# Attention's output matrix by seven products on pairs of node tiles, in a graph transformer on one Trainium2 core

## What is computed

```
for i in range(4):
    y = norm(x) * (1 + cond @ s1_w + s1_b) + cond @ b1_w + b1_b
    q, k, v = y @ wq + bq, y @ wk + bk, y @ wv + bv
    attn = softmax over the edges of q . k / sqrt(128), head by head
    x = x + (attn @ v) @ wo + bo
    y = norm(x) * (1 + cond @ s2_w + s2_b) + cond @ b2_w + b2_b
    x = x + relu(y @ m_w1 + m_b1) @ m_w2 + m_b2
```

## Time and profile before

| | us |
|---|---|
| median of 3 runs | 2349.93 (2349.65 to 2351.52) |
| the profiled execution's own time | 2344.98 |
| its span, first to last instruction | 2343.3 |
| TensorE busy | 2319.4 (99%) |
| VectorE busy | 1399.7 (60%) |
| ScalarE busy | 939.6 (40%) |
| GpSimd busy | 1098.8 (47%) |

### The profile page before, as it was taken

The page is one execution under the profiler, slowest core; times in us unless marked ns, Lnnn a source line. Parts: engine busy times, 40 slices in busy tenths (PEclk is TensorE's granted clock), DMA queues, the critical chain, the costliest instruction groups (busy, mean ns, idle before and its releaser), DMA issues. The chain is left out here.

```text
span 2343.3 us, 28395 instructions
## 1 busy us (share of the span) xinstructions
PE 2319.4 (99%) x9765; PEld 1465.6 (63%) x9765; DVE 1399.7 (60%) x2463; ACT 939.6 (40%) x1590; POOL 1098.8 (47%) x1482
## 2 busy tenths in 40 slices
PE   8999999999999999999999999999999999999999
PEld 4565655457676577777577777667767755544443
DVE  7777860524775663777564577565477655633445
ACT  4436642222764231666231376322266522312221
POOL 2005212041665481565384365466266543627775
PEclk9999999999999999999999999999999999999999
DMA  6411011420666210466210176510066611669517
GB/s 174 146 38 29 31 33 35 118 86 1 167 167 181 95 60 1 103 168 161 84 44 23 42 175 162 137 44 23 1 152 168 173 46 53 228 235 344 190 46 238
DMA packets 132367, 257.73 MB, mean 110 GB/s; under 512 B 49695, under 2 KB 51471, under 8 KB 129884
## 3 DMA queue, kind: packets, MB, share of 16 engines
q1 hardware_dynamic: 85294, 150.84, 21.7%
q0 software_dynamic: 45584, 102.75, 15.8%
q10 hardware_dynamic: 1346, 2.33, 0.4%
HBM read 213.17 MB, written 32.20 MB: 105 GB/s over the span
## 5 line engine op out<-in xcount | busy, mean ns | idle before, releaser
L115 POOL DMA_DIRECT2D cols<-w x720 | 354.1, 499 | 247.4 <-PE psum L1027 200.8
L1027 PE MATMUL psum<-cols,rows 125*128 125x256 f32 x1600 | 369.0, 379 | 0.0
L1014 PE MATMUL psum<-g_k_cols,g_q_cols 128*125 128x512 f32 (+1 forms) x960 | 360.8, 513 | 0.2
L1027 PEld LDWEIGHTS psum<-cols,rows 125*128 125x128 f32 x1600 | 303.2, 190 | 39.4 <-issue 3.8
L1133 DVE CUSTOM_DVE_ANT_0 g_prob<-psum,ln_count 125x1250 f32<-125x1250 f32 x160 | 233.8, 1461 | 101.3 <-PE psum L1014 100.9
L1014 PEld LDWEIGHTS psum<-g_k_cols,g_q_cols 128*125 128x125 f32 x960 | 179.4, 187 | 165.2 <-issue 155.5
L1231 ACT ACTIVATE g_prob<-g_prob,g_row_max 125x1250 f32<-125x1250 f32 x160 | 216.1, 1351 | 123.0 <-DVE g_row_max L1133 121.1
L1147 DVE STREAM_TRANSPOSE w<-g_prob 128x1280 f32<-128x1280 f32 x160 | 241.5, 1510 | 39.5 <-DMA cols<-w 26.8
L1237 ACT ACTIVATE g_prob<-g_prob,g_row_max 125x1250 f32<-125x1250 f32 x160 | 215.9, 1349 | 68.5 <-DVE g_row_max L1122 68.1
L3298 PE MATMUL psum<-m_ew,m_x_cols 128*64 128x256 f32 (+1 forms) x576 | 152.3, 498 | 0.0
L1040 PE MATMUL psum<-g_wo,g_q_cols 128*125 128x512 f32 x320 | 143.5, 593 | 0.0
(11 more groups left out here) (440 smaller groups left out, 4252.4 us busy)
## 6 DMA issues: line engine op xcount, KB each, us to landing
cols<-w POOLq DMA_DIRECT2D x720, 80.0 KB, 3.2
cols<-w SPq DMA_DIRECT2D x560, 80.0 KB
w<-in_L_gnn_m_w SPq DMA_DIRECT2D x8, 1024.0 KB
slot_rows<-p_kf SPq DMA_DIRECT2D x1, 7344.0 KB, 33.0
rows<-slot_rows SPq DMA_DIRECT2D x54, 136.0 KB
m_ew<-in_L_ffn_expert_w SPq DMA_DIRECT2D x4, 1536.0 KB, 12.6
slot_outputs<-slot_rows SPq DMA_DIRECT2D x1, 5000.0 KB
w<-in_L_mix_W SPq DMA_DIRECT2D x4, 1024.0 KB, 5.2
```

Of the source, the lines that this page charges most:

```text
L115: return eng.dma_start(out, in_, allow_slow_non_contiguous=True)
L1014: ins = pe.matmul(psum[0:P, at:at + width], q_cols[:, h, t * P:(t + 1) * P], k_cols[:, h, start:start + width], start=True, stop=True)
L1027: ins = pe.matmul(c.bank(6 + g % 2, 256).rearrange("p (u a i) -> p u a i", u=2, a=SIDE), rows[0:P, j, h * 128:(h + 1) * 128], turned_keys[ ...
```

## The change

`outputs` goes. `att_pe` takes its place in all four layers: the seven products of `mlp_pe`, on `wo`, with the attention's result in `q_cols` as the stationary side. The functions `mlp_*` that served the pairs are renamed `pair_*` and take a record, `att` or `mlp`, with the semaphores and the scratch; their work is the same. The norm behind attention follows the pairs' order (`by_pairs`), by `pair_stats_dve` and `apply_dve`. Sums of blocks are new: GpSimd makes those of `wo` behind the moves of pairs 11 to 14, and the first of each of two groups of node blocks behind those of 15 and 16; VectorE makes the rest for pair 0 ahead of the last transposition, for pairs 1 and 2 behind it; GpSimd makes those of pairs 3 and 4 after the parts of pairs 0 and 1. The sums of `m_w1` move behind the parts of pairs 2 and 3. `weigh` of pairs 18 and 19 stand in a row behind pair 0.

```diff
+    ATT_SUMS_AT = [(0, 0), (1, 0), (1, 1), (0, 0), (1, 0)]
+        k_all = k_cols[:].rearrange("p c n -> p (c n)")
+        att_weight_sums = [k_all[:, i * D:(i + 1) * D].rearrange("p (c o) -> p c o", c=2) for i in range(3)]
+        att_weight_sums.append(wo[:, 0:2, half_tile:D])
+        att_sums = [k_all[:, at:at + 8 * n].rearrange("p (i c n) -> p i c n", i=4, c=2)
+                    for at, n in ((3 * D, P), (3 * D + 8 * P, 2 * P))]
+        att = Pairs(0, o_mm, o_act_made, o_dve_made, o_pool_made, (0, 256, 512, 768, 1024, 1792, 2048, 2304))
+        mlp = Pairs(1, m_mm, m_act_made, m_dve_made, m_pool_made, range(0, 4 * D, half_tile))
...
-            return m % 2 == 1 and m < 2 * L - 1
+            return m < 2 * L - 1
...
+        def att_weight_sum_pool(l, n):
+            g = c.pool
+            a11, a21, a12, a22 = (wo[:, c0:c0 + 2, o:o + half_tile] for c0 in (0, 2) for o in (0, half_tile))
+            s1, s2, s3, s4 = att_weight_sums
+            if n == 0:
+                g.wait_ge(wo_in, 16 * KC * (l + 1))
+                g.tensor_tensor(s1, a21, a22, ALU.add).then_inc(o_weight_sums, 1)
...
+        def att_blocks(t0, t1, tiles=1):
+            return (q_cols[:, c0:c0 + 2, t * P:(t + tiles) * P] for c0 in (0, 2) for t in (t0, t1))
+        def att_first_sum_pool(l, slot):
+            g = c.pool
+            b11, b12, _, _ = att_blocks(slot, 3 + slot, 1 + slot)
+            if slot == 1:
+                g.wait_ge(out_made, PAIRS * l + PAIRS // 2)
+            g.tensor_tensor(att_sums[slot][:, 0], b12, b11, ALU.subtract).then_inc(o_sums_pool, 1)
+        def att_sums_dve(l, slot):
+            v = c.dve
+            _, b12, b21, b22 = att_blocks(slot, 3 + slot, 1 + slot)
+            t1, t2, t3, t4 = (att_sums[slot][:, i] for i in range(4))
+            v.wait_ge(out_made, PAIRS * l + NT // 2 * 3 + 2 + slot)
+            v.wait_ge(o_sums_pool, 10 * l + 2)
+            v.tensor_tensor(t2, b22, t1, ALU.subtract).then_inc(o_sums_dve, 1)
+            v.tensor_tensor(t3, b22, b12, ALU.subtract).then_inc(o_sums_dve, 1)
+            v.wait_ge(o_sums_dve, 6 * l + 3 * slot + 1)
+            v.tensor_tensor(t4, b21, t2, ALU.subtract).then_inc(o_sums_dve, 1)
+        def att_sums_pool(l, j):
+            g = c.pool
+            done = 10 * l + 4 * j - 10
+            b11, b12, b21, b22 = att_blocks(*VALUE_TILES[j])
+            t1, t2, t3, t4 = (att_sums[j - 3][:, i, :, 0:P] for i in range(4))
...
+        def att_pe(l, j, p):
+            pe = c.pe
+            n = VALUE_PAIRS * l + j
+            if p == 1:
+                if j == 0:
+                    pe.wait_ge(wo_in, 16 * KC * (l + 1))
+                    pe.wait_ge(score_read, STEPS * (l + 1) - 1)
+                    pe.wait_ge(out_made, PAIRS * l + NT // 2 * 3 + 2)
+                else:
+                    pe.wait_ge(o_act_made, 4 * n - 2)
+            elif p == 6:
+                if j == 0:
+                    pe.wait_ge(o_weight_sums, 4 * l + 4)
+                else:
+                    pe.wait_ge(o_dve_made, 3 * n)
+                if j < 2:
+                    pe.wait_ge(o_sums_dve, 6 * l + 3 * j + 3)
+                elif j >= 3:
+                    pe.wait_ge(o_sums_pool, 10 * l + 4 * j - 6)
+            elif p == 5 and j < 2:
+                pe.wait_ge(out_made, PAIRS * l + (PAIRS - 2 if j == 0 else PAIRS))
+            elif p == 7:
+                pe.wait_ge(o_dve_made, 3 * n + 1)
+            elif p == 3:
+                pe.wait_ge(o_act_made, 4 * n + 3)
...
+            ins.then_inc(o_mm, 1)
...
-            def outputs(t):
-                pe.wait_ge(out_made, PAIRS * l + 3 * NT // 2 + t // 2 + 1)
-                if t < 2:
-                    pe.wait_ge(score_read, STEPS * (l + 1) - 1)
-                else:
-                    pe.wait_ge(o_added, NT * l + t - 1)
-                for k in range(KC):
-                    ins = pe.matmul(c.bank(t % 2, D, P), q_cols[:, k, t * P:(t + 1) * P], wo[:, k, :],
-                                    start=(k == 0), stop=(k == KC - 1))
-                ins.then_inc(o_mm, 1)
-
...
-            pe.wait_ge(wo_in, 16 * KC * (l + 1))
-            outputs(0)
-            outputs(1)
-            weigh(PAIRS - 2, 0)
-            weigh(PAIRS - 2, 1)
-            pe.wait_ge(score_read, STEPS * (l + 1))
-            norm_pe(2 * l, 0)
-            norm_pe(2 * l, 1)
-            outputs(2)
-            weigh(PAIRS - 1, 0)
-            weigh(PAIRS - 1, 1)
-            for t in range(3, NT):
-                outputs(t)
-                if t == 3:
-                    pe.wait_ge(out_made, PAIRS * (l + 1))
-                norm_pe(2 * l, t - 1)
-            norm_pe(2 * l, NT - 1)
+            for j in range(VALUE_PAIRS):
+                for p in PAIR_ORDER:
+                    att_pe(l, j, p)
+                    if j >= 1 and p in (3, 4):
+                        norm_pe_turn(2 * l, 2 * j - (2 if p == 3 else 1))
+                if j == 0:
+                    pe.wait_ge(score_read, STEPS * (l + 1))
+                for t in (2 * j, 2 * j + 1):
+                    norm_pe_start(2 * l, t)
+                if j == 0:
+                    weigh(PAIRS - 2, 0)
+                    weigh(PAIRS - 2, 1)
+                    pe.wait_ge(o_dve_made, 3 * VALUE_PAIRS * l + 2)
+                    weigh(PAIRS - 1, 0)
+                    weigh(PAIRS - 1, 1)
...
+            att_sums_dve(l, 0)
             turn_squares(STEPS - 1)
-            v.wait_ge(bo_added, NT * (l + 1))
-            for t in range(NT + 1):
-                if t < NT:
-                    v.wait_ge(o_mm, NT * l + t + 1)
-                    v.tensor_tensor(x[:, t, :], x[:, t, :], c.bank(t % 2, D, P), ALU.add).then_inc(o_added, 1)
-                    v.wait_ge(o_added, NT * l + t + 1)
-                if t == 1:
-                    v.wait_ge(weighed, PAIRS * (l + 1))
-                norm_dve(2 * l, t)
+            att_sums_dve(l, 1)
+            for j in range(VALUE_PAIRS):
+                if j >= 1:
+                    pair_stats_dve(att, l, j - 1)
+                    if j == 1:
+                        v.wait_ge(weighed, PAIRS * (l + 1))
+                    apply_dve(2 * l, 2 * j - 2)
+                pair_u2_dve(att, l, j)
+                if j >= 1:
+                    apply_dve(2 * l, 2 * j - 1)
+                pair_ends_dve(att, l, j)
+            pair_stats_dve(att, l, VALUE_PAIRS - 1)
+            for t in (NT - 2, NT - 1):
+                apply_dve(2 * l, t)
...
-            take_out(PAIRS - 2)
-            take_out(PAIRS - 1)
-
-            for t in range(NT):
-                norm_act(2 * l, t)
+            for j in range(VALUE_PAIRS):
+                if j < 2:
+                    s.wait_ge(squared, STEPS * (l + 1) - 1 + j)
+                if j >= 2:
+                    std_act(2 * l, 2 * j - 2)
+                pair_first_act(att, l, j)
+                if j >= 2:
+                    std_act(2 * l, 2 * j - 1)
+                pair_block_act(att, l, j)
+                pair_last_act(att, l, j)
+                if j == 0:
+                    s.activation(row_max[:, 0, 1:2], ident[0:P, 0:1], ACT.Sqrt)
+                    take_out(PAIRS - 2)
+                    std_act(2 * l, 0)
+                    std_act(2 * l, 1)
+                    take_out(PAIRS - 1)
+                else:
+                    turned_act(2 * l, 2 * j - 2)
+                    turned_act(2 * l, 2 * j - 1)
+            for t in (NT - 2, NT - 1):
+                std_act(2 * l, t)
...
-            if l < L - 1:
-                g.wait_ge(squared, STEPS * (l + 1))
-                for n, value in ((1, 0.0), (3, 0.0), (0, 1.0), (2, 1.0)):
-                    g.memset(cond_w[n * SQUARE:(n + 1) * SQUARE, :], value).then_inc(ones_made, 1)
-                g.wait_ge(ones_made, 4 * (l + 1))
-            g.wait_ge(w_in[1], 16 * (2 * l + 2))
-            weight_sums_pool(w[1], h_store, weight_sums, h_run(l))
+                elif NT <= t < NT + 4:
+                    att_weight_sum_pool(l, t - NT)
+                elif NT + 4 <= t < NT + 6:
+                    att_first_sum_pool(l, NT + 5 - t)
+            g.wait_ge(bo_added, NT * (l + 1))
+            for j in range(VALUE_PAIRS):
+                pair_x_pool(att, l, j)
+                if j == 0 and l < L - 1:
+                    g.wait_ge(squared, STEPS * (l + 1))
+                    g.wait_ge(o_pool_made, 6 * (VALUE_PAIRS * l + 1))
+                    for n, value in ((1, 0.0), (3, 0.0), (0, 1.0), (2, 1.0)):
+                        g.memset(cond_w[n * SQUARE:(n + 1) * SQUARE, :], value).then_inc(ones_made, 1)
+                    g.wait_ge(ones_made, 4 * (l + 1))
+                if j < 2:
+                    att_sums_pool(l, j + 3)
+                elif j < 4:
+                    g.wait_ge(w_in[1], 16 * (2 * l + 2))
+                    weight_sums_pool(w[1], h_store, weight_sums, h_run(l), (j - 2,))
-                    g.wait_ge(o_mm, NT * (l + 1))
```

(40 more changed lines are left out.)

160 lines of the change are left out of this document (75 added, 85 removed).

## The result

The changed kernel takes 2355.95 us (median of ten runs, 2350.91 to 2359.15) and the kernel before 2349.75 (ten runs, 2346.22 to 2351.52). The ratio is 1.0028, with a 95% interval of 1.0018 to 1.0038: **slower by 0.28%**. The forecast was 2348.4 with a range up to 2354.0. The time lies outside it, and the kernel became slower where a small gain was forecast. The profiled execution took 2353.41 us with a span of 2351.7, against 2344.98 and 2343.3. On another chip the two kernels gave 2348.73 and 2341.26, ratio 1.0030 (1.0019 to 1.0040).

The account below looks back on a forecast made before the run. TensorE's own columns were taken to bound the kernel. 2344.98 less 14.4 us of gain plus three waits of 4.3 gave 2343.5 us profiled, 2348.4 as a median; 8-in-10 range 2335.5 to 2354.

Parts of the forecast that it names:

- The bound: Attention's end, first output matmul to the next product's first: TensorE's own columns set the end, 51.03 us in layer 0.
- The gain: Attention's end: new stretch 47.49 us against 51.03; 3.6 us less a layer taken, 14.4 in four, bounds 3.2 and 3.8.
- The covers at the start: Start of attention's end: weighing of pair 19 begins 11.2 us in, 0.9 us left at the least; costed at nothing.
- The new wait: Product 4 after attention, layers 0 to 2: TensorE waits 4.3 us each, as VectorE's nine operations alternate with GpSimd's sums.
- the two cases: Product 4's wait, by who gets in first at +8.0 us: 4.0 us if VectorE, 5.1 if GpSimd.
- the tie at +8.0: 8.0 us after the next product's first matmul, VectorE's fourth sum and GpSimd's first half-1 sum want the way together.
- the later case: GpSimd goes first at +8.0 us: last cast ends at +16.8, TensorE's wait at product 4 is 5.1 us.
- Rival 1: VectorE's nine operations hold off GpSimd; product 4 waits nothing or at most 2 us; median 2335.5 to 2341.5; chance 0.20.
- rival 2: Each of VectorE's nine is held by a whole GpSimd operation; product 4 waits 7.0 us; median 2356.5; chance 0.10.
- rival 3: Last squares come late: weighing of pair 19 waits up to 1 us a layer; median 2352.4; chance 0.05.
- Rival 4: Clock halves in TensorE's wait at product 4: three parts cost 3.8 us more a layer; median 2359.9; chance 0.05.
- The sum: Whole kernel: 2344.98 - 14.4 + 3 x 4.3 = 2343.5 us for the profiled execution, 2348.4 on the medians' scale.

Follow-up runs that it names:

- the filled wait: Changed kernel with 7 more TensorE products in front of product 4 of the first half, layers 0 to 2: ratio 0.9996 to the kernel before.

## Why the prediction was wrong, step by step

**The bound: right.** TensorE's own columns set the end in the stretch that was changed: with fewer columns, though 60 more records, it became 4.1 us shorter, busy throughout before and after. The 2.5 ns a matmul that I named in the prediction stand in the Trainium skill (TensorE: Matmul & The Clock Gate) under "Wait — 56ns, not 53.3ns?" and not under the heading that I gave; no run here isolates them.

**The gain: right in kind, 0.5 us a layer too small.** I put 47.49 us for the new stretch, took 3.6 us of gain and allowed up to 3.8. It was 46.96, a gain of 4.07. Pair 0 took 6.91 us and the two weighings 8.63, both as written. The four other pairs took 31.42 and not 31.94. The term at fault is the MLP's second pair. I read its wait of 0.22 us in the earlier trace rows and thought that 0.22 would go with it at most. The pair's own length showed more: 832.77 to 841.10 is 8.33 us, the next pair's 7.85. Attention's second pair took 7.86. So an idle time of 0.22 had cost 0.47. Of the other 0.25, some 0.16 is how the bracket is counted: from the end of the row ahead, and a row of four records shows 1.03 us while the next starts after 0.86. The records behind took 0.1 longer (four in 1.13 us). In all 16.3 us and not 14.4.

**The covers at the start: right.** No wait on the weighings in any layer. SyncE's load behind the moves, in layers 0 and 1 of the kernel after:

```profile
755.11 0.94 SPq L117 DMA_DIRECT2D w<-in_L_gnn_m_w  x2
...
1130.53 0.94 SPq L117 DMA_DIRECT2D w<-in_L_gnn_m_w  x2
```

That is 9.5 and 9.0 us behind the stretch's start, ahead of the 11.2 at which the weighing of pair 19 begins.

**The new wait: right in place and cause, near in number.** Three waits, none in layer 3, at the line named, of 4.8 us where 4.0 or 5.1 was worked out and 4.3 taken, so inside the two cases and 0.5 off the value taken. GpSimd's first sum started at T0 (792.57, T0 at 792.59). The last cast ended at +16.9, where 15.7 or 16.8 stood; the tie at +8.0 fell to GpSimd in all three layers, by 0.01 to 0.02 us (GpSimd's L366 at 800.61, VectorE's L723 at 800.63 in layer 0). I should have carried the later case. As a start delay it is 4.94 us a layer, 14.8 in all, against 12.9 in the sum. The Trainium skill (SBUF — State Buffer, "Who interferes with whom") holds as far as it goes: whoever issues first has the pair for the whole instruction (L718 ended 0.55 us behind the end of GpSimd's L369). Which waiter is next, which it does not say, was one of the other engine's each time. Rival 1 (VectorE keeps the way) is excluded by the block sums between its operations, rival 2 by 4.8 us instead of 7.0, rival 3 by the weighings. That rival 2's time, 2356.5, lies 0.6 us from the measured median is chance: it has no lower clock in it and 2.2 us more of wait in each layer.

**The clock: the step that failed.** Rival 4, "the clock falls in the wait", stood apart from the forecast with a chance of 0.05; the sum had the three waits and put what they do to the records behind them at nothing. The rival was no alternative to the forecast but followed from it: a wait of 4 to 5 us was forecast in three places, and what an idle TensorE does to its clock was then no longer a separate case. I gave it little because no row showed such a wait behind a busy stretch. That the trace before is silent is no evidence either way, and the term belonged in the sum with bounds of 0 and 3.8 us. Measured, it is 2.59, 2.40 and 2.21 us a layer, 7.2 in all, of which the filled wait gave back 6.9. The price in the rival, 3.8, was too high: only the eight records of product 4, two parts, ran at the lower clock, and not three. The rule of the Trainium skill that I cited there (TensorE: Matmul & The Clock Gate, "What's actually happening", an idle array falls to 1.2 GHz) is what the trace shows: 0.81 in the idle stretch, 0.51 behind it.

**The sum.** From 2343.5 to the 2353.4 of the profiled execution: clock +7.2, wait +1.9, gain -1.9, rest of the stretch +0.3, start and end of the kernel +2.4. That is 9.9. On the medians' scale the miss was 7.55 us, 2.4 less, since the median after lies 2.54 above its profiled execution and not the 4.95 that I carried over from before. I take the kernel's start and end to average out there, which is not shown; then the clock alone is nearly all of the miss, as wait and gain were off by the same 1.9 in opposite ways. With the clock at 2.4 and the later case of the tie, the forecast would have been about 2358. That the wait's error hid the gain's is luck.

**Range and chances.** "Slower" had 0.15, "same" 0.59. Since 0.2% is 4.7 us and the forecast stood 1.4 us below before, a term of 7 us left out was enough to change the sign.

## What to carry to other kernels

When a forecast contains a new idle time of the bounding engine, price at once what follows from it: the records behind the wait, not only the wait. Before moving row work between VectorE and GpSimd queues, put both queues side by side in time and count each VectorE sum or cast on SBUF that a GpSimd operation would overlap, bias additions included; where they alternate, operations of 0.4 to 0.7 us cost 1.2 to 2.3. The remedy is then cheap: three operations written behind the step that TensorE waits for gave back nearly everything, while nine moved to another crowded place cost 36 us against the kernel before. And take a stall's price from the length of the whole piece (8.33 against 7.85 us), not from the idle time in brackets (0.22).

## What was not expected of the hardware

- VectorE and GpSimd take turns even when VectorE's next operation depends on nothing: with a GpSimd operation between each two, nine of VectorE took 14.9 us that take about 5.3 undisturbed (an estimate: 798.75 to 803.61 and a cast). VectorE's additions with one input in PSUM were not held: L467 took 0.54 us beside GpSimd's bias additions, just behind a cast of 1.37.
- After 4.8 us idle behind a busy stretch the eight records of 375 columns took 4.3 to 5.1 us, and after 6.1 us idle 4.0 to 5.2, against 2.52. In the idle stretch itself the granted clock is given as 0.81 in one run and, for the same wait, as 1.00 in another, with 0.60 in the 4.32 us behind; the records behind are what tells.
- After 8.4 us idle the clock was at 0.53 for 6.5 us, and after 3.8 us idle soon behind that, at 0.62 over the next 3.4 us. What decides how long the lower clock lasts stays open; no run here varied it alone.
- At full clock a wait costs more than the idle time in brackets: with 0.39 us the eight records behind took 2.63 us and not 2.52, and with 0.22 us a piece grew by 0.47, of which some 0.16 is the way the bracket is counted.
